# A fused Mamba and mixture-of-experts layer: the skip term moved from TensorE to VectorE, the expert ranking moved one turn earlier, and two GpSimd jobs exchanged

## The chip, the cores and the metric

The kernel runs on one NeuronCore of one Trainium2 chip, in float32 throughout. The metric is the device time in microseconds (us). Before the change the median of three runs is 1366.08 us (1365.59 to 1366.9).

## The reference, cut to what matters

Two sequences of 2048 tokens with 256 channels go through a Mamba block, a gated feed-forward, and eight experts of which each token uses the best two.

```python
u  = layernorm(layernorm(x)) * ln1_w + ln1_b
xm, z = split(u @ in_proj_w.T)                  # 512 channels each
xc = silu(causal_conv4(xm) + conv_b)
dt, Bm, Cm = split(xc @ x_proj_w.T)             # 128, 16 and 16 columns
dt = softplus(dt @ dt_proj_w.T + dt_proj_b)
for t in time:                                  # h: 512 channels x 16 states
    h = h * exp(dt[t] * A) + dt[t] * Bm[t] * xc[t]
    y[t] = sum over states of h * Cm[t]
y = (y + xc * D_skip) * silu(z)
x1 = x + y @ out_proj_w.T
x2 = x1 + (silu(gate) * a) @ ff_out_w.T         # a, gate from layernorm(x1) @ ff_proj_w.T
p = softmax(router logits); the two largest p of a token, over their sum, weigh its experts
out = x2 + sum over e of w[e] * (n @ Wa[e] @ Wb[e])   # n = layernorm(x2); residual terms left out here
```

## The kernel before, in words

The tokens are cut into 16 steps (c, b) of 256 tokens: 8 chunks of each of the 2 sequences. A step has 16 turns, one for each state s. Five stages of five neighbouring steps are interleaved in every turn: `enter` (normalisation, input projection, convolution) and `ready` (step sizes, softplus, dt times x) of the steps to come, `main` (the scan) of the present one, `back` (output projection, feed-forward) and `tail` (routing, experts) of the two that have gone by. `drive` (line 152) writes that order out for each engine: `main` part 0, then the other stages in an order that each engine's `drive` call names, then `main` part 1. A loop covers steps (2, 0) to (5, 1); what precedes the first step is `opening`, what follows the last is `closing`. Nothing is planned at run time; each engine follows its own list and waits on semaphores.

A state s passes through the engines so. ScalarE makes dA = exp(dt A) (`decay`, L801), and ScalarE or, for the states in `POOL_STATES`, GpSimd multiplies uTs by B (`weigh_u`, L789 and L559) three turns ahead. TensorE transposes that into one of three PSUM banks `psx` (`fill_bx`, L1185, 4 transposes for each half). VectorE scans (L976, two instructions a half; half 0 in part 0 and half 1 in part 1). GpSimd multiplies the scanned h by C into `hC`, a ring of 4 (L575). TensorE transposes and adds `hC` into `psy` two turns later (`sum_states`, L1204).

The skip term xc times D is made by ScalarE four products at a time into `acc` (`skip`, L771), and TensorE starts the sum in `psy` with it in turn 2 (`add_skip`, L1195). After the last state VectorE multiplies `psy` by silu(z) (`ygt`, L987, in `back` 2), TensorE transposes the result in turn 3 (L1273) into `psb` and `pst`, ScalarE copies both halves to `yg` (L841, turns 3 and 4), and TensorE projects it in turns 4 and 5 (L1068). Before TensorE may write `psb` in turn 3, ScalarE must have copied half of z out of it (L820, `main` turn 3).

The ranking of the experts: VectorE makes the logits less their maximum in `tail` 2 (lgm, L1021), ScalarE their exponential pr in `tail` 3 (L873), GpSimd ten small instructions in `tail` 3 (L616 to L641, the last writes psel), VectorE the sum and its reciprocal in `tail` 4, ScalarE the weights cw in `tail` 4 (L878), TensorE their transposes in `tail` 4 (L1298). In turns 6 to 9 TensorE makes the hidden values of two experts each (`hidden`, L1062 into `pst`), and VectorE multiplies each pair out of `pst` (L1032, turns 7 to 10); the next pair may be written only then.

Softplus is relu plus log1p(exp(-|.|)) with a correction of log1p: VectorE's L960 and L962 (`ready` 8), then on GpSimd a subtraction (L542, `ready` 8), an addition (L547, `ready` 9) and the product with xc (L551, `ready` 10). GpSimd also normalises the coming input into `xn` in `enter` 6 (L510).

Of the kernel before, what the change touches and what calls it, by code (L numbers as in the profile page):

```python
# [8 lines left out]
P = 128  # L9
T = 256  # L10
SUB = T // P
# [14 lines left out]
EPS = 1e-5  # L26
NORM_FLOOR = 1e-12
LIFT = 20
POOL_STATES = (4, 8, 14, 15)


C_CONVW, C_CONVB, C_DTB, C_DSKIP, C_ALOG = 0, NJ * TAPS, NJ * TAPS + NJ, NJ * TAPS + 2 * NJ, NJ * TAPS + 3 * NJ
# [12 lines left out]


RANK_PARTS = 9
LINKS_IN = 1
LINKS_BACK = 2
LINKS_TAIL = 2  # L50
# [132 lines left out]
def mamba_moe(nc, x, params, w_in, w_x, w_dt, w_out, w_ff, w_fo, w_a, w_b, w_r, bc_scratch, cw_scratch, out):  # L183
# [9 lines left out]
    with ctx:  # L193
# [86 lines left out]

        u = sp_l
        hg = yg
        sk = acc

        def pairs(half):
            return nx[:, half, 0:SUB * NE * NE].rearrange("p (j e f) -> p j e f", j=SUB, e=NE)
# [7 lines left out]
        pst = ctx.enter_context(nc.psum_tensor("pst", [P, 2, T], f32))  # L297

        loaded = {k: sem(f"loaded_{k}") for k in ("par", "in", "x", "dt", "out", "ff", "fo", "a", "b", "r")}
        ident_zero, ident_ready, skip_ready = sem("ident_zero"), sem("ident_ready"), sem("skip_ready")  # L300
        earlier_one, earlier_ready = sem("earlier_one"), sem("earlier_ready")
        consts_ready, state_zero, halo_zero = sem("consts_ready"), sem("state_zero"), sem("halo_zero")
        a_exp, a_ready, ln_one_ready = sem("a_exp"), sem("a_ready"), sem("ln_one_ready")
# [157 lines left out]
        def _(pool):  # L461
# [74 lines left out]

            def ready(s, m):
                b = m[1]
                if s == 8:

                    pool.wait_ge(sp_fix, count(1, m, 1))
                    nc.gpsimd.tensor_tensor(sp_l[:, :, :], sp_l[:, :, :], sp_e[:, :, :], ALU.subtract  # L542
                                            ).then_inc(sp_rest, 1)
                if s == 9:
                    pool.wait_ge(relu_done, count(2, m, 2))
                    pool.wait_ge(sp_rest, count(1, m, 1))
                    nc.gpsimd.tensor_tensor(dt[:, b], dt[:, b], sp_l[:, :, :], ALU.add).then_inc(dt_done, 1)  # L547
                if s == 10:
                    pool.wait_ge(dt_done, count(1, m, 1))
                    pool.wait_ge(xc_done, count(1, m, 1))  # L550
                    nc.gpsimd.tensor_tensor(u[:, :, :], dt[:, b], xc[:, b], ALU.mult).then_inc(u_done, 1)  # L551
# [45 lines left out]
            def tail(s, m):  # L597
                if s == 0:
# [6 lines left out]
                    pool.wait_ge(nrm_part, squared)  # L605
                    nc.gpsimd.tensor_scalar(nrm[:, 2, :], nrm[:, 1, :], float(DM), NORM_FLOOR * NORM_FLOOR, ALU.mult,
                                            ALU.max).then_inc(nrm_done, 1)
                if s == 3:


                    if is_first(m):
                        pool.wait_ge(earlier_ready, 1)
                    pool.wait_ge(pr_done, count(1, m, 1))
                    p_j = pr[:, :, :].unsqueeze(2).to_broadcast([P, SUB, NE, NE])
                    p_e = pr[:, :, :].unsqueeze(3).to_broadcast([P, SUB, NE, NE])
                    nc.gpsimd.tensor_tensor(gap, p_j, p_e, ALU.subtract).then_inc(rank_part, 1)  # L616
                    differed = value(count(RANK_PARTS, m, 1))
                    pool.wait_ge(ident_ready, 1)
                    pool.wait_ge(rank_part, differed)
                    nc.gpsimd.tensor_scalar(ahead, gap, 0.0, None, ALU.is_equal).then_inc(rank_part, 1)  # L620
                    nc.gpsimd.tensor_scalar(gap, gap, 0.0, None, ALU.is_gt).then_inc(rank_part, 1)
                    pool.wait_ge(rank_part, count(RANK_PARTS, m, 3))
                    nc.gpsimd.tensor_tensor(ahead, ahead, earlier[:, :, :].unsqueeze(1).to_broadcast([P, SUB, NE, NE]),
                                            ALU.mult).then_inc(rank_part, 1)
                    pool.wait_ge(rank_part, count(RANK_PARTS, m, 4))
                    nc.gpsimd.tensor_tensor(ahead, ahead, gap, ALU.add).then_inc(rank_part, 1)
                    pool.wait_ge(rank_part, count(RANK_PARTS, m, 5))
                    nc.gpsimd.tensor_tensor(ahead[:, :, :, 0:4], ahead[:, :, :, 0:4], ahead[:, :, :, 4:8], ALU.add
                                            ).then_inc(rank_part, 1)
                    pool.wait_ge(rank_part, count(RANK_PARTS, m, 6))  # L630
                    nc.gpsimd.tensor_tensor(ahead[:, :, :, 0:2], ahead[:, :, :, 0:2], ahead[:, :, :, 2:4], ALU.add
                                            ).then_inc(rank_part, 1)
                    pool.wait_ge(rank_part, count(RANK_PARTS, m, 7))
                    nc.gpsimd.tensor_tensor(rank[:, :, :], ahead[:, :, :, 0], ahead[:, :, :, 1], ALU.add
                                            ).then_inc(rank_part, 1)
                    ranked = value(count(RANK_PARTS, m, 8))
                    pool.wait_ge(ident_ready, 1)
                    pool.wait_ge(rank_part, ranked)
                    nc.gpsimd.tensor_scalar(rank[:, :, :], rank[:, :, :], 1.5, None, ALU.is_lt).then_inc(rank_part, 1)
                    pool.wait_ge(rank_part, count(RANK_PARTS, m, 9))  # L640
                    nc.gpsimd.tensor_tensor(psel[:, :, :], rank[:, :, :], pr[:, :, :], ALU.mult).then_inc(psel_done, 1)  # L641
# [4 lines left out]
        def _(act):  # L646
# [29 lines left out]
            def enter(s, m):  # L676
# [11 lines left out]
                    last.then_inc(uT_done, 1)  # L688
                if s in (4, 5):
                    i = s - 4  # L690
                    act.wait_ge(skip_added, count(1, m, -1))
                    act.wait_ge(filled_in, in_fill(f"x{i}", m))
                    for k in range(2):
                        j = 2 * i + k
# [7 lines left out]
                                         ).then_inc(halo_kept, 1)  # L702
                if s == 10:

                    act.wait_ge(edge_added, count(1, m, 1))
                    nc.scalar.activation(xc[:, b, :, :], acc[:, :, :], ACT.Silu).then_inc(xc_done, 1)
                    if isinstance(m[0], int) and m[0] == 0:
                        use_log_exp()
                if s == 12:
# [1 line left out]
                    act.wait_ge(filled_in, in_fill("bc", m))  # L711
                    nc.scalar.activation(bc[:, :], (pst if is_first(m) else psf)[0:2 * S, 1, :], ACT.Copy
                                         ).then_inc(bc_done, 1)
                if s == 12 and is_early(m) and not is_first(m):
                    skip(prev(m))

            def ready(s, m):
                b = m[1]
# [27 lines left out]
                if s == 8:  # L746
# [3 lines left out]
                    src = psb if is_first(m) else psf  # L750
                    nc.scalar.activation(sz[:, b, 1, :], src[:, :, :].rearrange("p k t -> p (k t)"), ACT.Copy
                                         ).then_inc(z1_copied, 1)
                if s == 12 and not is_first(m):
                    skip(m)
                if s in (13, 14):

                    j = s - 13
# [4 lines left out]
                    nc.scalar.activation(uTs[:, b, j, :], src, ACT.Copy).then_inc(uTs_done, 1)  # L762
                if s >= 13:
                    made(s - S, m)

            def skip(m):


                act.wait_ge(xc_done, count(1, m, 1 if is_last(m) else 2))
                for j in range(NJ):  # L770
                    last = nc.scalar.activation(sk[:, j, :], xc[:, m[1], j, :], ACT.Copy, scale=pcol(C_DSKIP + j))  # L771
                last.then_inc(skip_ready, 1)

            def made(turn, n):

# [85 lines left out]
            def tail(s, m):  # L861
# [3 lines left out]
                if s == 1:  # L865
# [2 lines left out]
                    nc.scalar.activation(lnn[:, :], nrm[:, 2, :], ACT.Ln, scale=float(2 ** LIFT)).then_inc(lnn_done, 1)  # L868
                    act.wait_ge(lnn_done, count(1, m, 1))
                    nc.scalar.activation(rn[:, :], lnn[:, :], ACT.Exp, scale=-0.5, bias=lift_c[:, :]).then_inc(rn_done, 1)  # L870
                if s == 3:
                    act.wait_ge(lgm_done, count(1, m, 1))
                    nc.scalar.activation(pr[:, :, :], lgm[:, :, :], ACT.Exp).then_inc(pr_done, 1)  # L873
                if s == 4:
# [7 lines left out]
                    act.wait_ge(cw_stored, count(16, m, 0))  # L882
                    nc.scalar.activation(cT[:, :], pst[0:NE, 0, :], ACT.Copy).then_inc(cT_done, 1)

            drive(act, {"else": ("tail", "back", "ready", "enter")}, enter, ready, main, back, tail)

        @block.vector
        def _(dve):
# [67 lines left out]
            def ready(s, m):  # L956
                if s == 8:

                    dve.wait_ge(sp_ln, count(1, m, 1))
                    nc.vector.scalar_tensor_tensor(out=sp_l[:, :, :], in0=sp_l[:, :, :], scalar=ln_one[:, :],  # L960
                                                   in1=sp_e[:, :, :], op0=ALU.subtract, op1=ALU.add)
                    nc.vector.tensor_scalar(sp_e[:, :, :], sp_e[:, :, :], 1.0, -1.0, ALU.add, ALU.add  # L962
                                            ).then_inc(sp_fix, 1)

            def main(s, n, part):
                b, r = n[1], ring(s)
                if part == 0:
                    dve.wait_ge(exp_done, count(S, n, s + 1))

# [72 lines left out]
        def _(pe):  # L1042
# [143 lines left out]
                                                   bxT[:, ring(s), j, c:c + P], ident[:, :])  # L1186
                last.then_inc(bx_filled, 1)

            def add_skip(n):

                pe.wait_ge(skip_ready, count(1, n, 1))
                pe.wait_ge(yg_done, count(2, n, 0))
                for j in range(SUB):
                    for i in range(NJ):
                        last = mm(psy[j][:, i * P:(i + 1) * P], sk[:, i, j * P:(j + 1) * P], ident[:, :],  # L1195
                                  is_transpose=True, start=i == 0, stop=False, skip_group_check=True)
                last.then_inc(skip_added, 1)

            def sum_states(s, n):

                pe.wait_ge(hc_done, count(S, n, s + 1))
                for j in range(SUB):
                    for i in range(NJ):
                        last = mm(psy[j][:, i * P:(i + 1) * P], hC[:, s % RC, i, j * P:(j + 1) * P], ident[:, :],  # L1204
                                  is_transpose=True, start=False, stop=s == S - 1, skip_group_check=True)
                last.then_inc(y_summed, 1)

            def main(s, n, part):
# [3 lines left out]
                    pe.wait_ge(eT_done, count(1, n, -1))  # L1212
                    gate_inputs(psb, 0, n[1]).then_inc(z0_filled, 1)
                if part == 1:
                    if s == 2:
                        add_skip(n)
                    if s >= 2:
                        sum_states(s - 2, n)

# [161 lines left out]
```

## Time and profile before

| | us |
|---|---|
| median of 3 runs | 1366.08 |
| the profiled execution | 1364.54 |
| its span, first to last instruction | 1362.8 |
| TensorE busy | 1231.1 (90%) |
| TensorE weight loads busy | 1058.5 (78%) |
| VectorE busy | 971.3 (71%) |
| ScalarE busy | 1057.8 (78%) |
| GpSimd busy | 1092.7 (80%) |
| mean granted TensorE clock | 0.976 of full |

Busy time is the time in which an engine executes something. Five overlapping stages keep all engines busy, so the shares tell little by themselves; what matters is which wait ends last in a turn. In the middle of the kernel a step takes 78.6 to 80.2 us and repeats itself closely.

### The profile page before, as it was taken

How to read it: one execution, taken by the hardware profiler on the slowest of the kernel's cores; microseconds unless marked ns; L12 is line 12 of the kernel's file. 1: busy time of each engine (PE TensorE's matmuls, PEld its weight loads, DVE VectorE, ACT ScalarE, POOL GpSimd, SP SyncE). 2: the span in 40 equal slices, each digit the busy share in tenths (PEclk: the TensorE clock that was granted, in tenths of full speed). 3: DMA queues.
4: the chain of work that ended last, by engine and by line, in shares of the span. 5: the costliest groups of instructions: out<-in, count | busy, mean ns of one | idle time of the engine just before them, and what ended most of it. 6: DMA issues, size and time to landing. Idle time of an engine off the chain costs nothing.

```text
span 1362.8 us, 24300 instructions
## 1 busy us (share of the span) xinstructions
PE 1231.1 (90%) x7680; PEld 1058.5 (78%) x7680; DVE 971.3 (71%) x1765; ACT 1057.8 (78%) x2537; POOL 1092.7 (80%) x826
## 2 busy tenths in 40 slices
PE   4587889999999999999999999999999999898986
PEld 3366777887878787787878878787887878787875
DVE  2486868778786876878687786868778686878621
ACT  3798898888787878878788887878788787878420
POOL 3389798888888888888888888888888888788721
PEclk8798899999999999999999999999999999999998
DMA  1411102111121111112111111211121021202001
GB/s 65 171 47 40 39 26 77 40 47 63 48 79 46 57 40 56 56 48 79 49 56 40 66 46 48 79 48 56 40 79 47 33 71 48 71 24 73 30 32 47
DMA packets 29223, 75.08 MB, mean 55 GB/s; under 512 B 3104, under 2 KB 15776, under 8 KB 26528
## 3 DMA queue, kind: packets, MB, share of 16 engines
q1 hardware_dynamic: 29088, 73.41, 16.1%
q8 instruction: 69, 1.13, 0.3%
q14 instruction: 66, 0.54, 0.1%
HBM read 64.61 MB, written 4.59 MB: 51 GB/s over the span
## 4 chain that ended last, share of the span: by engine, by line
PE 72%; ACT 9%; DVE 7%; issue 5%; POOL 2%; DMA 0%; DVEq 0%; ACTq 0%; POOLq 0%; SPq 0%
PE psx L1185 12%; PE psy L1204 12%; PE psb L1062 8%; PE psb L1068 8%; PE pst L1068 8%; PE pst L1062 6%; DVE h L976 3%; ACT dA L801 2%; PE psf L1062 2%; ACT bxT L789 2%; PE psf L1153 2%; PE psf L1159 2%; PE psf L1094 2%; PE psb L1159 2%; PE psf L1105 2%
## 5 line engine op out<-in xcount | busy, mean ns | idle before, releaser
L976 DVE TENSOR_TENSOR_SCAN h<-dA,state,psx 128x256 f32<-128x256 f32 x1024 | 681.4, 726 | 112.8 <-PE psx L1185 99.2
L575 POOL TENSOR_TENSOR hC<-h,bC 128x1024 f32<-128x1024 f32 x256 | 606.1, 2372 | 96.0 <-DVE h L976 73.8
L801 ACT ACTIVATE dA<-dt,neg_a 128x256 f32<-128x256 f32 x1024 | 434.3, 500 | 0.0
L1185 PE MATMUL psx<-ident,bxT 128*128 128x128 f32 x2048 | 307.0, 276 | 25.2 <-DVE h L976 15.2
L789 ACT ACTIVATE bxT<-uTs,BT 128x512 f32<-128x512 f32 x384 | 254.1, 717 | 67.4 <-PE psx L1185 65.8
L1185 PEld LDWEIGHTS psx<-ident,bxT 128*128 128x128 f32 x2048 | 246.2, 143 | 68.5 <-issue 24.3
L1204 PE MATMUL psy<-ident,hC 128*128 128x128 f32 x2048 | 267.6, 274 | 1.5 <-POOL hC L575 1.5
L1204 PEld LDWEIGHTS psy<-ident,hC 128*128 128x128 f32 x2048 | 235.2, 143 | 4.5 <-POOL hC L575 1.7
L559 POOL TENSOR_TENSOR bxT<-uTs,BT 128x1024 f32<-128x1024 f32 x64 | 121.5, 1898 | 32.0 <-PE psx L1185 32.0
L1062 PE MATMUL psb<-nT,w_ff_sb 128*128 128x256 f32 x496 | 121.8, 388 | 12.9 <-ACT yg L814 11.7
L1062 PE MATMUL pst<-eT,w_a_sb 128*128 128x256 f32 x448 | 107.2, 382 | 14.2 <-DVE cbc L1032 14.2
L1062 PEld LDWEIGHTS psb<-nT,w_ff_sb 128*128 128x128 f32 x496 | 89.3, 190 | 34.7 <-ACT yg L814 18.0
L1068 PE MATMUL pst<-w_b_sb,cbc 128*128 128x256 f32 x480 | 110.8, 379 | 0.0
L1062 PEld LDWEIGHTS pst<-eT,w_a_sb 128*128 128x128 f32 x448 | 81.8, 190 | 26.5 <-DVE cbc L1032 15.6
L1068 PEld LDWEIGHTS pst<-w_b_sb,cbc 128*128 128x128 f32 x480 | 90.1, 190 | 11.7
L483 POOL TENSOR_SCALAR nx<-x,mv,rstd 128x256 f32<-128x256 f32 x64 | 77.6, 1223 | 22.9 <-ACT rstd L662 22.9
L1068 PE MATMUL psb<-w_out_sb,yg 128*128 128x256 f32 x256 | 65.8, 402 | 26.3 <-ACT yg L841 26.3
L952 DVE SCALAR_TENSOR_TENSOR acc<-psf,par,acc 128x255 f32<-128x255 f32 (+1 forms) x180 | 73.6, 472 | 17.3 <-ACT halo L701 17.3
L1068 PEld LDWEIGHTS psb<-w_out_sb,yg 128*128 128x128 f32 x256 | 49.1, 197 | 38.6 <-ACT yg L841 30.6
L999 DVE TENSOR_TENSOR yg<-yg,psb 128x512 f32<-128x512 f32 x31 | 21.3, 688 | 66.3 <-PE psb L1062 66.3
L542 POOL TENSOR_TENSOR sp_l<-sp_l,sp_e 128x1024 f32<-128x1024 f32 x16 | 37.8, 2363 | 35.5 <-DVE sp_e L962 35.5
L1062 PE MATMUL psf<-uT,w_in_sb 128*128 128x256 f32 x240 | 60.0, 394 | 4.7 <-ACT uT L686 2.5
(148 smaller groups left out, 1633.7 us busy)
## 6 DMA issues: line engine op xcount, KB each, us to landing
bC<-bc_scratch SPq DMA_DIRECT2D x64, 512.0 KB, 3.8
cbc<-cw_scratch SPq DMA_DIRECT2D x16, 1024.0 KB, 4.7
xf<-in_x SPq DMA_DIRECT2D x16, 256.0 KB, 2.7
xk<-xn SPq DMA_DIRECT2D x16, 256.0 KB, 4.3
xb<-in_x SPq DMA_DIRECT2D x16, 256.0 KB, 4.2
out<-x SPq DMA_DIRECT2D x16, 256.0 KB, 2.2
w_in_sb<-in_w_in SPq DMA_DIRECT2D x1, 1024.0 KB, 5.2
w_ff_sb<-in_w_ff SPq DMA_DIRECT2D x1, 1024.0 KB, 5.9
```

Of the source, the lines that this page charges most:

```text
L483: last = nc.gpsimd.tensor_scalar(dst[:, j, :], src[:, j, :], mv[k][:, j, 0:1], rstd[k + 1][:, j:j + 1], ALU.subtract, ALU.mult)
L559: nc.gpsimd.tensor_tensor(bxT[:, ring(s)], uTs[:, n[1]], BT[:, n[1], :, s:s + 1].to_broadcast([P, SUB, DI]), ALU.mult).then_inc(bxT_pool, 1)
L575: nc.gpsimd.tensor_tensor(hC[:, s % RC], h[:, ring(s)], bC[:, g % RINGG, s % G:s % G + 1, :].to_broadcast([P, NJ, T]), ALU.mult).then_inc( ...
L789: last = nc.scalar.activation(bxT[:, ring(s), j, :], uTs[:, n[1], j, :], ACT.Copy, scale=BT[:, n[1], j, s:s + 1])
L801: last = nc.scalar.activation(dA[:, s % RA, j, :], dt[:, n[1], j, :], ACT.Exp, scale=neg_a[:, j, s:s + 1])
L952: nc.vector.scalar_tensor_tensor(out=acc[:, j, tap:], in0=x_bank(i, m)[:, j % 2, 0:T - tap], scalar=pcol(C_CONVW + j * TAPS + k), in1=acc[ ...
L976: last = nc.vector.tensor_tensor_scan(h[:, r, j, :], dA[:, s % RA, j, :], psx[bx_bank(fill)][:, k, :], state[:, b, j, s:s + 1], ALU.mult, ...
L1062: last = mm(dst[:, i, :], w[:, k, c:c + P], rhs[:, k, :], start=k == 0, stop=k == kt - 1)
L1068: last = mm(dst[:, j, :], lhs[:, k, j * P:(j + 1) * P], w[:, k, :], start=k == 0, stop=k == kt - 1)
L1159: last = mm(dst[:, :, :].rearrange("p k t -> p (k t)"), uT[:, b, k, j * P:(j + 1) * P], w_in_sb[:, k, DI:2 * DI], start=k == 0, stop=k == ...
L1185: last = nc.tensor.transpose(psx[bx_bank(fill)][:, k, j * P:(j + 1) * P], bxT[:, ring(s), j, c:c + P], ident[:, :])
L1204: last = mm(psy[j][:, i * P:(i + 1) * P], hC[:, s % RC, i, j * P:(j + 1) * P], ident[:, :], is_transpose=True, start=False, stop=s == S - ...
```

## The change

`POOL_STATES` gets state 6: GpSimd makes its bxT and ScalarE no longer does. ScalarE's `skip` and TensorE's `add_skip` go; the first state's sum starts `psy`. VectorE adds xc times D to `hC` of state 4, in place, in part 1 of turn 6, ahead of its scans, and TensorE's sum of state 4 waits for it. VectorE does the subtraction of softplus in `ready` 9. `tail` 3 of ScalarE and GpSimd (pr and the ranking) becomes `tail` 2, and ScalarE's order of the stages changes in turns 2 and 4.

```diff
-POOL_STATES = (4, 8, 14, 15)
+POOL_STATES = (4, 6, 8, 14, 15)
+SKIP = 4
...
 (GpSimd, ready)
-                if s == 8:
-                    pool.wait_ge(sp_fix, count(1, m, 1))
-                    nc.gpsimd.tensor_tensor(sp_l[:, :, :], sp_l[:, :, :], sp_e[:, :, :], ALU.subtract
-                                            ).then_inc(sp_rest, 1)
 (GpSimd, tail; ScalarE, tail)
-                if s == 3:
+                if s == 2:
 (ScalarE, enter)
                 if s in (4, 5):
-                    act.wait_ge(skip_added, count(1, m, -1))
+                    act.wait_ge(xc_done, count(1, m, 0))
                 if s == 10:
+                    act.wait_ge(skip_added, count(1, m, -1))
-                if s == 12 and is_early(m) and not is_first(m):
-                    skip(prev(m))
 (ScalarE, ready; skip itself goes too)
-                if s == 12 and not is_first(m):
-                    skip(m)
 (ScalarE)
-            drive(act, {"else": ("tail", "back", "ready", "enter")}, ...)
+            drive(act, {2: ("back", "ready", "enter", "tail"), 4: ("back", "tail", "ready", "enter"),
+                        "else": ("tail", "back", "ready", "enter")}, ...)
 (VectorE, ready)
+                if s == 9:
+                    dve.wait_ge(sp_fix, count(1, m, 1))
+                    nc.vector.tensor_tensor(sp_l[:, :, :], sp_l[:, :, :], sp_e[:, :, :], ALU.subtract).then_inc(sp_rest, 1)
 (VectorE, main, first thing)
+                if part == 1 and s == SKIP + 2:
+                    dve.wait_ge(hc_done, count(S, n, SKIP + 1))
+                    for j in range(NJ):
+                        last = nc.vector.scalar_tensor_tensor(out=hC[:, SKIP % RC, j, :], in0=xc[:, b, j, :],
+                                                              scalar=pcol(C_DSKIP + j), in1=hC[:, SKIP % RC, j, :],
+                                                              op0=ALU.mult, op1=ALU.add)
+                    last.then_inc(skip_added, 1)
 (TensorE; add_skip and its call in turn 2 go)
             def sum_states(s, n):
+                if s == 0:
+                    pe.wait_ge(yg_done, count(2, n, 0))
+                if s == SKIP:
+                    pe.wait_ge(skip_added, count(1, n, 1))
...
-                                  is_transpose=True, start=False, stop=s == S - 1, skip_group_check=True)
+                                  is_transpose=True, start=s == 0 and i == 0, stop=s == S - 1, skip_group_check=True)
```

## Rows read from the trace of the kernel before

**Rows 1.** Part 4 of the page: shares of the chain that ended last.

```profile
PE 72%; ACT 9%; DVE 7%; issue 5%; POOL 2%; DMA 0%; DVEq 0%; ACTq 0%; POOLq 0%; SPq 0%
```

**Rows 2.** Waits of the run: engine line <- releaser: us in total, times, longest.

```profile
PE psb L1068 <- ACT yg L841: 26.3, 16, 3.2
...
PE pst L1062 <- DVE cbc L1032: 14.2, 12, 1.2
```

**Rows 3.** Timeline of TensorE, one step: start us, us, engine line op [idle before].

```profile
766.86 1.04 PE L1195 MATMUL psy<-ident,acc 128*128 128x128 f32 x8
767.73 1.04 PE L1204 MATMUL psy<-ident,hC 128*128 128x128 f32 x8
...
769.48 0.60 PE L1273 MATMUL psb<-ident,ygt 128*128 128x128 f32 x4
...
772.10 1.89 PE L1062 MATMUL psf<-uT,w_in_sb 128*128 128x256 f32 x8
775.57 1.99 PE L1068 MATMUL psb<-w_out_sb,yg 128*128 128x256 f32 x8 [1.58 <-ACT yg L841]
...
789.73 1.99 PE L1062 MATMUL pst<-eT,w_a_sb 128*128 128x256 f32 x8 [1.20 <-DVE cbc L1032]
```

**Rows 4.** Timeline of ScalarE, same step.

```profile
768.72 0.61 ACT L820 ACTIVATE sz<-psb 128x512 f32<-128x512 f32 x1
...
771.60 1.33 ACT L789 ACTIVATE bxT<-uTs,BT 128x512 f32<-128x512 f32 x2
772.83 1.70 ACT L801 ACTIVATE dA<-dt,neg_a 128x256 f32<-128x256 f32 x4
...
774.94 0.57 ACT L841 ACTIVATE yg<-pst 128x512 f32<-128x512 f32 x1
```

**Rows 5.** Timeline of GpSimd, same step.

```profile
763.42 2.38 POOL L575 TENSOR_TENSOR hC<-h,bC 128x1024 f32<-128x1024 f32 x1
...
769.63 0.39 POOL L616 TENSOR_TENSOR nx<-pr 128x128 f32<-128x128 f32 x1
...
773.82 0.22 POOL L641 TENSOR_TENSOR psel<-rank,pr 128x16 f32<-128x16 f32 x1
...
778.64 1.90 POOL L559 TENSOR_TENSOR bxT<-uTs,BT 128x1024 f32<-128x1024 f32 x1
...
783.15 2.45 POOL L510 TENSOR_SCALAR xn<-xf,mv,rstd 128x256 f32<-128x256 f32 x2
```

**Rows 6.** Timeline of VectorE, same step.

```profile
765.12 0.72 DVE L1021 TENSOR_TENSOR lgm<-lg,mx 128x16 f32<-128x16 f32 x1
...
783.17 0.69 DVE L992 TENSOR_TENSOR x<-xk,psb 128x512 f32<-128x512 f32 x1 [1.24 <-PE psb L1068]
...
784.87 1.65 DVE L952 SCALAR_TENSOR_TENSOR acc<-psf,par,acc 128x255 f32<-128x255 f32 x4
786.45 2.65 DVE L976 TENSOR_TENSOR_SCAN h<-dA,state,psx 128x256 f32<-128x256 f32 x4
789.01 0.66 DVE L1032 TENSOR_TENSOR cbc<-cbc,pst 128x512 f32<-128x512 f32 x1
```

**Rows 7.** Line 960 in the whole run: ns minimum/median/maximum, first and last start.

```profile
L960 DVE SCALAR_TENSOR_TENSOR sp_l<-sp_l,ln_one,sp_e x16: 1269/2642/3369, 37.3 to 1185.2; 128x1024 f32<-128x1024 f32 x16
```

**Rows 8.** Timeline of VectorE, then of TensorE, turns 9 to 11 of another step.

```profile
721.06 2.65 DVE L976 TENSOR_TENSOR_SCAN h<-dA,state,psx 128x256 f32<-128x256 f32 x4
...
725.34 0.60 PE L1185 MATMUL psx<-ident,bxT 128*128 128x128 f32 x4
```

**Rows 9.** A stretch: us, busy PE PEld DVE ACT POOL, granted clock, DMA share, GB/s.

```profile
220.00:224.00 4.00, 3.87 (x15) 3.17 (x16) 3.89 (x9) 4.00 (x12) 3.24 (x2) 0.67 0.42 134
```

**Rows 10.** Timeline of TensorE at two of its longer waits.

```profile
220.13 2.61 PE L1068 MATMUL psb<-w_out_sb,yg 128*128 128x256 f32 x8 [2.00 <-ACT yg L841]
...
1169.85 3.40 PE L1068 MATMUL psb<-w_out_sb,yg 128*128 128x256 f32 x8 [3.21 <-ACT yg L841]
```

**Rows 11.** A group: line engine op xcount, busy us, mean ns, idle before, releaser.

```profile
L542 POOL TENSOR_TENSOR sp_l<-sp_l,sp_e 128x1024 f32<-128x1024 f32 x16 | 37.8, 2363 | 35.5 <-DVE sp_e L962 35.5
```

More of the change, by code:

```diff
@@ L285, in mamba_moe @@
         hg = yg
-        sk = acc
         def pairs(half):
@@ L299, in mamba_moe @@
         loaded = {k: sem(f"loaded_{k}") for k in ("par", "in", "x", "dt", "out", "ff", "fo", "a", "b", "r")}
-        ident_zero, ident_ready, skip_ready = sem("ident_zero"), sem("ident_ready"), sem("skip_ready")
+        ident_zero, ident_ready = sem("ident_zero"), sem("ident_ready")
         earlier_one, earlier_ready = sem("earlier_one"), sem("earlier_ready")
@@ L764, in ready @@
                     made(s - S, m)
[L766 to L772, printed above, removed]
             def made(turn, n):
@@ L870, in tail @@
                     nc.scalar.activation(rn[:, :], lnn[:, :], ACT.Exp, scale=-0.5, bias=lift_c[:, :]).then_inc(rn_done, 1)
-                if s == 3:
+                if s == 2:
                     act.wait_ge(lgm_done, count(1, m, 1))
@@ L883, in tail @@
                     nc.scalar.activation(cT[:, :], pst[0:NE, 0, :], ACT.Copy).then_inc(cT_done, 1)
-            drive(act, {"else": ("tail", "back", "ready", "enter")}, enter, ready, main, back, tail)
+            drive(act, {2: ("back", "ready", "enter", "tail"), 4: ("back", "tail", "ready", "enter"),
+                        "else": ("tail", "back", "ready", "enter")}, enter, ready, main, back, tail)
         @block.vector
@@ L1187, in fill_bx @@
                 last.then_inc(bx_filled, 1)
[L1189 to L1197, printed above, removed]
             def sum_states(s, n):
+                if s == 0:
+                    pe.wait_ge(yg_done, count(2, n, 0))
+                if s == SKIP:
+                    pe.wait_ge(skip_added, count(1, n, 1))
                 pe.wait_ge(hc_done, count(S, n, s + 1))
@@ L1214, in main @@
                 if part == 1:
-                    if s == 2:
-                        add_skip(n)
                     if s >= 2:
```

## The prediction

> **What bounds the kernel now.** I read the chain first. TensorE holds 72% of it and every other engine under a tenth [rows 1]: in the middle of the kernel TensorE's list is the path, and the others count where they make TensorE wait. The list of waits gives those places [rows 2]: 16 waits for ScalarE's copy of yg (26.3 us together) and 12 for VectorE's expert product (14.2 us). The timelines of one step show them again, 1.58 us in turn 4 and 1.20 us in turn 7 [rows 3].
>
> In turn 4 the copy of yg stands on ScalarE behind the expert weights, and these behind the ranking, which GpSimd ends at 774.04 [rows 4, 5]. In turn 7 the path goes the other way. TensorE's projection lets VectorE start its addition at 783.17; two normalisation statistics, four convolution taps, four scans and the expert product follow without a gap to 789.67, and TensorE goes on at 789.73 [rows 3, 6]. From 783.17 to 789.73 **VectorE is the path**. Whatever is put into that stretch is paid in full.
>
> I work in the time of this one step, which 12 of the 16 resemble (the 12 waits of [rows 2]).
>
> **Part by part.** *No skip transposes.* Eight transposes go; by the starts of their block and the next they hold TensorE 0.87 us [rows 3]. But three blocks later TensorE writes `psb`, from which ScalarE copies z from 768.72 to 769.33, and TensorE begins at 769.48 [rows 3, 4]: it was there just in time. ScalarE's list ahead of that copy is not shortened (its skip products stood in turn 12, state 6 in turn 3). So the 0.87 us becomes a new wait for L820: I count 0, and 0.87 at best. ScalarE's exponential now stands ahead of that copy and costs 0.1.
>
> *Ranking in turn 2, state 6 on GpSimd.* ScalarE loses bxT of state 6, 1.23 us from start to start [rows 4], and in turn 4 copies yg before the expert weights. It reaches the copy after dA at about 773.2 and ends it by 773.9. TensorE's input projection starts at 772.10 and, at 1.73 us a block of eight (the 0.16 is overlap), leaves it at 773.83. The wait of 1.58 shrinks to about 0.1. Gain: **1.5 us a step** (0 to 1.58).
> GpSimd's list grows here. The exponential is ready at 766.1, so the ten instructions, 4.4 us from 769.63 to 774.04 [rows 5], end at 770.6. Behind them queue hC of state 2, the new bxT of state 6 (1.86, as the one at 778.64), hC of 3 and 4 (2.33 each), bxT of 8, hC of 5, and then xn, two instructions of 1.2 us. Summed, xn runs from **783.65 to 786.05**, against 783.15 to 785.6 now. TensorE needs bxT of state 6 at 777.3 and has it at 774.9; it needs the product of state 2 at 776.5 and has it at 773.0. These are covered by over 2 us.
>
> *The skip on VectorE.* Four instructions, 256 elements each, one input scaled. The nearest row is four taps, 1.58 us by starts [rows 6], but a tap has one input in PSUM. With both in SBUF there is L960: 1269 ns at best for 1024 elements, 2642 in the middle [rows 7]. The difference is GpSimd: the subtraction lgm of 16 elements took 0.72 us and ended at 765.84, as the product of 763.42 did on GpSimd (765.80) [rows 5, 6]. A VectorE instruction with two SBUF inputs stands while GpSimd executes a tensor_tensor. No row shows it against a tensor_scalar, which xn is. Bounds: nothing blocks, 1.6 us; both halves of xn block, 1.6 + 2.4 = 4.0 us. The taps end at 786.45 - 1.5 = 784.95, xn at 786.05, so 1.1 us of blocking is the value I take, since xn too reads SBUF: **2.7 us a step**, all on the stretch where VectorE is the path.
> The Trainium skill, "SBUF — State Buffer", section "Who interferes with whom", says that a VectorE instruction with two SBUF inputs contends with a GpSimd instruction that reads SBUF, whichever it is, and that the later one blocks fully. Lgm agrees as to tensor_tensor; for tensor_scalar the page alone speaks. By it the block is the 1.1 us, without it 0.
> Queued behind the skip on VectorE are the scans of turn 6, and TensorE's sum of state 4, its next fills of `psx` and its expert block all wait.
>
> *Subtraction on VectorE.* 1024 elements from two SBUF inputs: 1.17 us free, up to 2.6 blocked [rows 7]. It delays the scans of [rows 8] from 721.06. Their first two would end 1.7 us later than 722.4, at 724.1, and TensorE asks for them at 725.34: hidden, by 1.2 us. The addition on GpSimd comes 0.2 us later than now. If that cover were gone it would cost up to 1.4 us a step. I take 0. GpSimd saves 2.36 us and its wait for L962 [rows 11], off the path.
>
> *Clock.* TensorE will stand for some 4 of 6 us around turn 6: 2.3 us for the skip, 0.4 for a scan, 1.6 for the expert product. Now it stands 1.20 and 1.58 us at a time, and the eight matmuls behind each take 1.99 us [rows 3]. After a stand of 2.00 us the same eight took 2.61, and the stretch from 220 shows a granted clock of 0.67, so partly the lower level of 1.2 GHz; after 3.21 us they took 3.40 [rows 9, 10]. Between 0 (the slow part falls into a stand) and 1.4 I take **0.6 us a step**.
>
> **The sum.** A middle step: 0.1 is within the 1.5, so -1.5 + 2.7 + 0 + 0.6 = +1.8, times 12 = +21.6. The others: in the opening ScalarE's four skip products (1.6 by starts, as the four dA of [rows 4]) and half of the subtraction (2.36 [rows 11] to 1.17) leave the path, -2.8. The first step pays the skip and saves the subtraction on GpSimd, +0.5; the second has a shorter wait for yg, and pays the skip, +1. The last two have no convolution: their waits for yg of 3.2 [rows 10] and about 2.7 (which [rows 2] leaves when the others are taken off) shrink to 0.7, the first with 1.4 of slow clock, and the skip costs 0.85 each: -3.0 and -1.2. Sum of these -5.5. Together **+16** on the profiled execution's 1364.54 (span 1362.8 and 1.7 around it), 1380.6; the median lay 1.5 above that execution, so 1382.
>
> **Rivals.**
> 1. *GpSimd's tensor_scalar does not block.* Then a step is -1.5 + 1.6 = +0.1 and the rest -5.5: -4, 1362, faster. With the clock's 0.6 it is +3, 1369. For it: no row shows such a block. Against: the operand side is the same as that of the blocking product. 0.23, half of it with the clock.
> 2. *VectorE has room.* The skip fits between other work, the transposes' 0.87 and the 1.5 are kept: -2.4 times 16, 1328. It needs slack on VectorE from 783.17 to 789.67, and there is none; decides if TensorE's wait in turn 7 does not grow. 0.05.
> 3. *The clock halves in each step, and both halves of xn block.* 1.3 and 0.8 more: +1.8 becomes +3.9, times 12 less 5.5 is +41, 1408. 0.07.
> 4. *Ranking ahead of state 2's product holds the scans.* VectorE's scan of state 5 could start at 772.6 and gets that product at 773.0. Were the list on GpSimd 3 us later, the taps of turn 5 and TensorE's input block behind them would be late and the gain of 1.5 lost: +1.5 times 12 on top, 1400. Against: by my sum these taps wait for ScalarE until 775.4, a second after the scan. 0.05.
> 5. *The change does less than it says*: ScalarE still reaches yg late and the skip is not blocked: like 1, no gain, +1.6 a step, 19 less 5.5 is +14, 1380. Near the forecast; 0.05.
>
> The forecast itself has 0.55: 1382; 1375 without the clock and 1392 with all of it bound it. A difference under 0.2% (2.7 us) can't be told from none in this kernel. Faster: half of rival 1, rival 2 and a rest for what I mis-sized, 0.21. Same: 0.1. Slower: 0.69. The range 1360 to 1400 takes in rival 1 and leaves out 2 and 3.
>
> **What would show it.** Right: turn 4's wait for L841 near 0.1; a new wait of TensorE for L820 of 0.8 in turn 3; the four skip instructions at 0.4 us each but the first of 1.5 us, while xn executes; TensorE's waits in turns 6 and 7 at 4 us together, and clock under 1 in some of these stretches; middle steps at 79.7 to 80.5 us instead of 78.7. Wrong: a middle step under 78.6 us; skip instructions of 0.4 us beside xn (rival 1); no longer wait in turn 7 (rival 2); VectorE's scan of state 5 waiting for GpSimd (rival 4).

## The result, and the profile after

| | before | after |
|---|---|---|
| median, us | 1366.49 (4 runs) | 1375.97 (4 runs) |
| profiled span, us | 1362.8 | 1373.6 |
| VectorE busy | 971.3 (71%) | 1033.2 (75%) |
| ScalarE busy | 1057.8 (78%) | 1014.7 (74%) |

The ratio is 1.0068, interval 1.005 to 1.0085: **slower, by 9.5 us**; forecast were 1382 and 1360 to 1400. One run of early_silu below took 1825.36 us at a granted clock of 0.652 and is left out of its figures. The shares of the chain, against [rows 1], have moved from TensorE to VectorE:

```profile
PE 61%; DVE 15%; ACT 9%; issue 8%; DMA 1%; POOL 1%; DVEq 0%; ACTq 0%; POOLq 0%; SPq 0%
```

The waits of the whole run (columns as in [rows 2]) say where. Of the 26.3 us for yg 2.0 are left, all in the last two steps and behind them, and 26.3 us for the skip stand in their place, one wait in each of the 16 steps; the wait for the expert product stays.

```profile
PE psy L1194 <- DVE hC L959: 26.3, 16, 2.8
PE psx L1181 <- DVE h L972: 17.0, 28, 2.5
PE pst L1058 <- DVE cbc L1028: 15.2, 14, 1.2
```

TensorE's timeline in the step of [rows 3], which now runs 2.4 us later as a whole:

```profile
772.15 0.63 PE L1261 MATMUL psb<-ident,ygt 128*128 128x128 f32 x4 [0.77 <-issue]
...
776.54 1.99 PE L1064 MATMUL psb<-w_out_sb,yg 128*128 128x256 f32 x8
...
787.48 0.60 PE L1181 MATMUL psx<-ident,bxT 128*128 128x128 f32 x4
789.54 1.09 PE L1194 MATMUL psy<-ident,hC 128*128 128x128 f32 x8 [1.46 <-DVE hC L959]
790.76 0.66 PE L1181 MATMUL psx<-ident,bxT 128*128 128x128 f32 x4
792.62 1.99 PE L1058 MATMUL pst<-eT,w_a_sb 128*128 128x256 f32 x8 [1.20 <-DVE cbc L1028]
```

The projection that waited 1.58 waits no more; the block of the skip's sum waits 1.46. The reader should also see what did not change: both eights of 256 columns take 1.99 us, as in [rows 3]. The 0.77 in front of L1261 is the z copy of the prediction, which the waits list as "issue": ScalarE's timeline ends that copy at 772.05, and TensorE starts at 772.15. Of ScalarE:

```profile
768.41 0.24 ACT L856 ACTIVATE pr<-lgm 128x16 f32<-128x16 f32 x1
...
771.44 0.61 ACT L803 ACTIVATE sz<-psb 128x512 f32<-128x512 f32 x1
...
775.90 0.59 ACT L824 ACTIVATE yg<-pst 128x512 f32<-128x512 f32 x1
```

VectorE's stretch of [rows 6], and GpSimd beside it, with the skip between the taps and the scans:

```profile
785.90 1.65 DVE L936 SCALAR_TENSOR_TENSOR acc<-psf,par,acc 128x255 f32<-128x255 f32 x4
787.47 1.94 DVE L959 SCALAR_TENSOR_TENSOR hC<-xc,par,hC 128x256 f32<-128x256 f32 x4
789.34 2.65 DVE L972 TENSOR_TENSOR_SCAN h<-dA,state,psx 128x256 f32<-128x256 f32 x4
791.91 0.66 DVE L1028 TENSOR_TENSOR cbc<-cbc,pst 128x512 f32<-128x512 f32 x1
...
786.16 2.46 POOL L509 TENSOR_SCALAR xn<-xf,mv,rstd 128x256 f32<-128x256 f32 x2
```

xn lies over the skip until 788.62, and the skip takes no more than 1.94 us; in the 12 middle steps it takes 1.79 to 2.16. Where no GpSimd instruction lies beside it, in the second step, it takes 1.67:

```profile
157.14 1.67 DVE L959 SCALAR_TENSOR_TENSOR hC<-xc,par,hC 128x256 f32<-128x256 f32 x4
```

The last two steps have no convolution, so VectorE comes to the skip while GpSimd executes two products, both tensor_tensor, L553 (which makes bxT) and then L569:

```profile
1179.76 4.37 DVE L959 SCALAR_TENSOR_TENSOR hC<-xc,par,hC 128x256 f32<-128x256 f32 x4
...
1178.67 1.90 POOL L553 TENSOR_TENSOR bxT<-uTs,BT 128x1024 f32<-128x1024 f32 x1
1180.52 2.53 POOL L569 TENSOR_TENSOR hC<-h,bC 128x1024 f32<-128x1024 f32 x1
...
1184.19 1.57 PE L1194 MATMUL psy<-ident,hC 128*128 128x128 f32 x8 [2.23 <-DVE hC L959]
...
1187.34 3.78 PE L1058 MATMUL pst<-eT,w_a_sb 128*128 128x256 f32 x8 [0.68 <-DVE cbc L1028]
```

Here the skip takes 2.7 us more than alone, and the eight matmuls after the two stands take 3.78 instead of 1.99: the granted clock from 1187 to 1191 is 0.50, so TensorE is at the lower of its two levels, 1.2 GHz instead of 2.4. In the last step the skip takes 4.34, and the eight after it 2.10. The mean granted clock from 1182 to 1305 is 0.96; from 1179 to 1295 of the kernel before it is 0.99.

Step by step (from one start of the z product on VectorE to the next) the spans' difference of 10.8 us is made up so:

| part | forecast | measured |
|---|---|---|
| opening and first step | -2.8 and +0.5 | +0.9 (135.79 to 136.70) |
| second step | +1 | +0.3 |
| the 12 middle steps | +21.6 | +3.7 (950.3 to 954.0) |
| last two steps | -3.0, -1.2 | +2.3, +2.0 |
| tail | not in the sum | +1.7 |
| sum | +16.1 | +10.8 (the parts are rounded) |

### The profile page after: what moved, and what is told of

Its sections match the earlier page's. It is cut to its first block, busy times and chain, and to the rows that moved or that the text cites. A ratio compares the mean times of both kernels' runs of the same rounds, so it can differ in the third digit from the quotient of the medians.

```text
span 1373.6 us, 24039 instructions
## 1 busy us (share of the span) xinstructions
PE 1222.1 (89%) x7552; PEld 1044.8 (76%) x7552; DVE 1033.2 (75%) x1845; ACT 1014.7 (74%) x2441; POOL 1087.2 (79%) x826
## 3 DMA queue, kind: packets, MB, share of 16 engines
q1 hardware_dynamic: 29088, 73.41, 16.1%
## 4 chain that ended last, share of the span: by engine, by line
PE 61%; DVE 15%; ACT 9%; issue 8%; DMA 1%; POOL 1%; DVEq 0%; ACTq 0%; POOLq 0%; SPq 0%
PE psx L1181 10%; PE psy L1194 10%; PE pst L1064 8%; PE psb L1064 7%; DVE h L972 7%; PE psb L1058 6%; PE psf L1058 3%; PE pst L1058 3%; ACT dA L784 3%; PE psf L1090 2%; PE psf L1149 2%; PE psf L1101 2%; DVE hC L959 2%; DVE acc L936 2%; PE psb L1155 1%
## 5 line engine op out<-in xcount | busy, mean ns | idle before, releaser
L569 POOL TENSOR_TENSOR hC<-h,bC 128x1024 f32<-128x1024 f32 x256 | 606.9, 2375 | 112.1 <-DVE h L972 108.7
L1194 PE MATMUL psy<-ident,hC 128*128 128x128 f32 x2048 | 270.4, 276 | 27.8 <-DVE hC L959 26.3
L772 ACT ACTIVATE bxT<-uTs,BT 128x512 f32<-128x512 f32 x352 | 232.8, 716 | 67.6 <-PE psx L1181 66.0
L553 POOL TENSOR_TENSOR bxT<-uTs,BT 128x1024 f32<-128x1024 f32 x80 | 151.9, 1899 | 28.1 <-PE psx L1181 28.1
L482 POOL TENSOR_SCALAR nx<-x,mv,rstd 128x256 f32<-128x256 f32 x64 | 77.6, 1221 | 24.6 <-ACT rstd L656 24.6
L791 ACT ACTIVATE state<-h 128x4 f32<-128x4 f32 x256 | 51.0, 205 | 30.6 <-DVE h L972 30.5
L753 ACT ACTIVATE uTs<-psf 128x512 f32<-128x512 f32 x30 | 17.9, 597 | 63.2 <-PE psf L1163 63.2
L541 POOL TENSOR_TENSOR dt<-dt,sp_l 128x1024 f32<-128x1024 f32 x16 | 37.8, 2362 | 29.7 <-DVE sp_l L950 29.7
```

What stands on the lines that cost most here:

```text
L482: last = nc.gpsimd.tensor_scalar(dst[:, j, :], src[:, j, :], mv[k][:, j, 0:1], rstd[k + 1][:, j:j + 1], ALU.subtract, ALU.mult)
L553: nc.gpsimd.tensor_tensor(bxT[:, ring(s)], uTs[:, n[1]], BT[:, n[1], :, s:s + 1].to_broadcast([P, SUB, DI]), ALU.mult).then_inc(bxT_pool, 1)
L569: nc.gpsimd.tensor_tensor(hC[:, s % RC], h[:, ring(s)], bC[:, g % RINGG, s % G:s % G + 1, :].to_broadcast([P, NJ, T]), ALU.mult).then_inc( ...
L772: last = nc.scalar.activation(bxT[:, ring(s), j, :], uTs[:, n[1], j, :], ACT.Copy, scale=BT[:, n[1], j, s:s + 1])
L791: nc.scalar.activation(state[:, n[1], :, s:s + 1], h[:, ring(s), :, T - 1:T], ACT.Copy).then_inc(state_saved, 1)
```

## The experiments

Ratios are against runs of the kernel before on the same chip, taken together with each experiment; their medians are 1364.3 to 1366.3 us, so two times of different experiments can differ by 2 us for that alone. A middle step is 78.7 us before and 79.05 after. In every kernel three to five of the twelve middle steps are 1 to 3 us longer; step times and ranges below are those of the others.

**undo_skip**: everything but the skip, which stays on ScalarE and TensorE.

```diff
-if part == 1 and s == SKIP + 2:     # VectorE: xc*D onto hC of state 4
+if s == 12 and not is_first(m): skip(m)   # ScalarE, and add_skip on TensorE
```

> The changed kernel with the skip term back on ScalarE and TensorE; the ranking in turn 2, state 6 on GpSimd and the subtraction on VectorE stay. Theory (the skip on VectorE is paid in full in turn 6, the rest gains some 1.5 us a step): TensorE's wait of about 1.4 us for the skip goes, the wait for yg stays away, a middle step 77.3 us against 78.7 before and 79.2 changed, and about 1343 us in all. Rival A (the three other edits bring nothing, what was gained in turn 4 came from shorter TensorE lists): 1366. Rival B (a part of the loss is the subtraction on VectorE): 1350 to 1360.

1345.76 (1343.76 to 1347.14), ratio 0.9865, 0.9849 to 0.9882. The rest of the change wins 18.6 us. A middle step takes 77.1 to 77.6, TensorE's waits in turn 4 of the middle steps and for the skip are gone, and what is left in turns 4 to 7 is the expert product's:

```profile
777.17 1.99 PE L1062 MATMUL pst<-eT,w_a_sb 128*128 128x256 f32 x8 [1.20 <-DVE cbc L1032]
```

Against the whole change the skip costs 30.2 us, and 28.0 if each time is taken against its own kernel before; by the two spans 28.2, of it 18.9 in the 12 middle steps (1.6 each), 4.5 in the last but one, 2.5 in the second, but only 0.2 in the last (67.19 to 67.37). There the step is 1.8 us longer than before (65.39) without any skip. VectorE's expert product waits there for the transfer that brings the expert weights, and TensorE for that product:

```profile
1232.83 0.69 DVE L1032 TENSOR_TENSOR cbc<-cbc,pst 128x512 f32<-128x512 f32 x1 [2.07 <-DMA cbc<-cw_scratch]
1233.57 2.75 PE L1062 MATMUL pst<-eT,w_a_sb 128*128 128x256 f32 x8 [1.93 <-DVE cbc L1032]
```

The kernel before has no such wait in that step, and the whole change has none either: there the skip takes up that time.

**skip_only**: the kernel before with the skip's move alone.

```diff
+if part == 1 and s == SKIP + 2:     # VectorE
-if s == 12 and not is_first(m): skip(m)
```

> The kernel before with nothing but the skip term on VectorE in turn 6. Theory: no gain in turn 4, as the copy of yg still waits for the ranking; the four instructions cost 1.6 to 1.9 us in each of the 12 middle steps, and the last two are not blocked by a product on GpSimd, since that one has ended: about 1390 us. TensorE still stands 0.8 us for the copy of z in turn 3. Rival (the skip transposes were worth their 0.87 us a step): 1377.

1394.89 (1389.77 to 1396.91), ratio 1.0223, 1.0196 to 1.0251. The skip costs 30.6 us without the others too. The totals agree within 2.5 us, but they are not made up of the same parts, so that they agree shows only that the skip's cost does not need the other edits. A middle step takes 80.25, 1.6 more than before (17.0 for the twelve). No skip is slowed here from the second step on: 1.66 or 1.67 us in each middle step, and 1.64 in the last two, where GpSimd's product has ended at 1201.90 as expected:

```profile
1202.34 1.64 DVE L960 SCALAR_TENSOR_TENSOR hC<-xc,par,hC 128x256 f32<-128x256 f32 x4
```

In exchange the opening with the first step is 3.7 us longer than before (139.44), the second step 2.7, and the last 3.6, with a wait for yg of 4.9 instead of 2.7.

**rank_only**: ranking in turn 2 with ScalarE's new orders, nothing else.

```diff
-if s == 3:
+if s == 2:
+drive(act, {2: ("back", "ready", "enter", "tail"), 4: ("back", "tail", "ready", "enter"), ...
```

> The kernel before with nothing but the ranking in turn 2 and ScalarE's new orders in turns 2 and 4; state 6 stays on ScalarE. Theory: ScalarE reaches the copy of yg only 0.3 to 0.4 us earlier, since its bxT of state 6 stands ahead of it, so the wait in turn 4 falls from 1.58 to about 1.2 us; more in the last two steps, whose waits of 3 us were the ranking's alone: about 1357 us. Rival (the ranking alone was the wait, state 6 is idle weight): wait near 0.1 and 1343.

1357.26 (1354.67 to 1357.93), ratio 0.9956, 0.994 to 0.9973. The wait for yg is 18.7 us in all where it was 26.3, 1.1 in a middle step instead of 1.5: ScalarE still makes bxT of state 6 ahead of it.

**state6_only**: state 6 on GpSimd, nothing else.

```diff
-POOL_STATES = (4, 8, 14, 15)
+POOL_STATES = (4, 6, 8, 14, 15)
```

> The kernel before with nothing but state 6 scaled by GpSimd. Theory (GpSimd makes it in turn 3 ahead of the ranking, whose end is what the copy of yg waits for): 1.9 us more of TensorE's wait in turn 4 in 14 steps, and a slow clock behind some of these waits: about 1393 us, 3.4 us of wait a step. Rival (ScalarE's relief counts more): 1350 to 1366.

1403.41 (1401.43 to 1405.37), ratio 1.0278, 1.0261 to 1.0295: slower than I expected by 10. GpSimd now makes bxT ahead of the ranking, and by that the ranking, the expert weights and yg end 1.9 us later. GpSimd, ScalarE and TensorE, turns 3 and 4:

```profile
788.44 1.90 POOL L559 TENSOR_TENSOR bxT<-uTs,BT 128x1024 f32<-128x1024 f32 x1
790.29 0.41 POOL L616 TENSOR_TENSOR nx<-pr 128x128 f32<-128x128 f32 x1
...
794.49 0.22 POOL L641 TENSOR_TENSOR psel<-rank,pr 128x16 f32<-128x16 f32 x1
...
795.21 0.49 ACT L879 ACTIVATE cw<-psel,rden 128x8 f32<-128x8 f32 x2 [3.12 <-DVE rden L1027]
795.61 0.57 ACT L842 ACTIVATE yg<-pst 128x512 f32<-128x512 f32 x1
...
796.24 2.70 PE L1069 MATMUL psb<-w_out_sb,yg 128*128 128x256 f32 x8 [3.46 <-ACT yg L842]
```

The wait is 3.46 instead of 1.58, and part of the time is the lower level behind it: 2.70 us here, and 3.78 one step earlier behind a stand of 2.87. Two stands of one length in this run show that the length alone does not settle it:

```profile
549.56 1.99 PE L1069 MATMUL psb<-w_out_sb,yg 128*128 128x256 f32 x8 [2.86 <-ACT yg L842]
...
879.10 3.62 PE L1069 MATMUL psb<-w_out_sb,yg 128*128 128x256 f32 x8 [2.86 <-ACT yg L842]
```

The granted clock is 1.00 from 549 to 551 and 0.55 from 879 to 882. So the same edit costs 38 us alone and, once the ranking stands ahead of it, gains 10 or more on top of rank_only (1345.8 to 1347.0 against 1357.3). Ranking and state 6 are one edit in two places.

**sub_only**: softplus' subtraction on VectorE, nothing else.

```diff
-nc.gpsimd.tensor_tensor(sp_l[:, :, :], sp_l[:, :, :], sp_e[:, :, :], ALU.subtract)
+nc.vector.tensor_tensor(sp_l[:, :, :], sp_l[:, :, :], sp_e[:, :, :], ALU.subtract)
```

> The kernel before with nothing but softplus' subtraction on VectorE. Theory: covered in every middle step (VectorE waits for TensorE in turns 10 to 12), 1.2 us less in the opening: within 2 us of before, 1363. Rival (VectorE's added 1.9 us a step reach TensorE in turns 9 and 10): 1370 or more.

1364.35 (10 runs, 1359.19 to 1368.17), ratio 0.9997, 0.9982 to 1.0012: no difference.

**undo_both**: undo_skip, with the subtraction on GpSimd again as well.

```diff
-if s == 9:  # VectorE
-    nc.vector.tensor_tensor(sp_l[:, :, :], sp_l[:, :, :], sp_e[:, :, :], ALU.subtract)
+if s == 8:  # GpSimd
+    nc.gpsimd.tensor_tensor(sp_l[:, :, :], sp_l[:, :, :], sp_e[:, :, :], ALU.subtract)
```

> Ranking in turn 2 and state 6 on GpSimd alone: both the skip and softplus' subtraction are as in the kernel before. Beside the run with only the skip undone (1345.8) it differs by where the subtraction runs. Theory: the subtraction's place is worth nothing (alone it measured 0.9997), so 1346 (1344 to 1348). Rival: with state 6 on GpSimd its queue is fuller, the subtraction there makes dt and the later hC late, 3 to 8 us slower: 1349 to 1354, with waits of psy for POOL hC.

1347.05 (1345.78 to 1348.83), ratio 0.9863, 0.9842 to 0.9884: nothing is seen of the subtraction's place on a fuller GpSimd either.

**skip7**: the whole change, with the skip one turn later, onto state 5.

```diff
-SKIP = 4
+SKIP = 5
```

> The changed kernel with the skip added to state 5's product, in turn 7 and so behind the expert product of that turn, instead of state 4's in turn 6. Theory (only the place on the path makes the skip dear): VectorE has some slack between turn 7 and turn 9, so a middle step loses 0.3 to 0.8 us of the skip's 1.9 and takes about 78.0 us; TensorE's wait for the skip in turn 6 goes: about 1356 us. Rival (VectorE's work counts wherever it stands): as the changed kernel, 1376.

1359.46 (10 runs, 1357.37 to 1361.02), ratio 0.9961, 0.9951 to 0.9972. One turn is worth 14 us by the spans (16.5 by the medians). A middle step takes 77.8 to 78.3, and the last two steps 70.64 and 66.08 where the whole change has 74.94 and 67.37. It costs 14 more than undo_skip, so turn 7 has no room for all of the skip either.

**skip7_z0**: skip7, and ScalarE copies the first half of z one turn earlier.

```diff
-if part == 0 and s == 3:
+if s == 2:      # in part 1, ahead of made
     nc.scalar.activation(sz[:, n[1], 0, :], psb..., ACT.Copy).then_inc(z0_copied, 1)
```

> The changed kernel with the skip in turn 7 on state 5's product, and ScalarE's copy of the first half of z in turn 2, ahead of that turn's scaling and decay, instead of in turn 3. Theory (the 0.87 us of the skip transposes were lost to that copy alone): TensorE's wait of 0.8 us in turn 3 goes, a middle step 77.4 us instead of 78.2, about 1347 us. Rival (the next wait on ScalarE, yg or the relu, takes its place): 1357 to 1360.

1356.3 (1354.67 to 1358.21), ratio 0.9932, 0.9915 to 0.9949. The wait of 0.8 for the copy is gone and a middle step gains only 0.2 on average. Two others on ScalarE stand in its place:

```profile
768.86 1.99 PE L1058 MATMUL psf<-uT,w_in_sb 128*128 128x256 f32 x8 [0.15 <-ACT uT L680]
771.03 1.99 PE L1064 MATMUL psb<-w_out_sb,yg 128*128 128x256 f32 x8 [0.18 <-ACT yg L824]
```

The expected 77.4 us a step and 1347 were wrong; the rival, other waits on ScalarE and 1357 to 1360, was near. These two make up 0.33 of the 0.8; the rest was not traced.

**undo_skip_z0**: the same copy in undo_skip.

> The changed kernel with the skip back on ScalarE and TensorE, and ScalarE's copy of the first half of z one turn earlier. Middle steps then wait only 2.4 for cbc, 1.4 for the gate product, 1.1 for ScalarE's bxT and 0.7 for scans in two steps; there is no wait for the z copy that the earlier copy could take away. Theory: no gain, 1346 (1343 to 1349), with another 0.5 to 1 us wait for bxT or a scan in a middle step since ScalarE's copy stands ahead of them. Rival: the copy still moves the turns behind it forward and each middle step gains 0.3 (as 0.2 to 0.3 in the pair with the skip in turn 7), 1342.

1341.84 (6 runs, 1338.02 to 1348.63), ratio 0.9823, 0.9797 to 0.9848: the fastest that was run, and faster than both kernels of this case. No gain was expected, and the rival's 1342 was met; but this interval ends where that of undo_skip begins, and 3.0 of the 4.6 us by which the middle steps of the two traces differ lie in one step (80.07 to 77.11), so how much the copy gives is not settled.

**early_silu**: the whole change, without the wait for the skip ahead of Silu in the two opening steps, where its count is 0.

```diff
-act.wait_ge(skip_added, count(1, m, -1))
+skips = count(1, m, -1)
+if not (isinstance(skips, int) and skips == 0):
+    act.wait_ge(skip_added, skips)
```

> The changed kernel with one wait less: in the two opening steps ScalarE does not wait for skip_added ahead of Silu (the count it waits for is 0 there, so nothing is ordered by it). Theory: with two waits ahead of Silu the activation table is loaded behind them, on the path (49.14 in the changed kernel, 43.52 in the kernel before, where it lay in the idle time before POOL's edge); with one wait the load goes back into the idle time. In the profile the loads then start near 18.9 and 43.5 us, and xc (Silu) follows its taps without 1.28 us between; the opening ends 1.3 to 2.5 us earlier, and the time is 1374 (1373 to 1375) against the changed kernel's 1376. Rival: the loads move, but the opening is held by something else (the weights' DMAs, the halved clock), and the time stays at 1376. Rival 2: the place of the load has nothing to do with the wait; loads stay at 49.1.

1373.44 (1371.08 to 1376.43), ratio 1.0054, 1.0034 to 1.0074, which is not told apart from the whole change. But the load of the activation table did move. ScalarE in the whole change, then here:

```profile
49.14 1.28 ACT L701 ACT_TABLE_LOAD   x1 [4.50 <-POOL acc L533]
50.43 1.06 ACT L701 ACTIVATE xc<-acc 128x1024 f32<-128x1024 f32 x1
```

```profile
44.44 1.28 ACT L703 ACT_TABLE_LOAD   x1
48.89 1.06 ACT L703 ACTIVATE xc<-acc 128x1024 f32<-128x1024 f32 x1 [3.17 <-POOL acc L533]
```

With a second wait ahead of the activation the load ran behind the wait, and with one it ran in the idle time before it, as it did in the kernel before (43.52). The activation comes 1.5 us earlier, and the opening ends 0.2 earlier (136.49): TensorE's wait for ScalarE's bxT falls from 9.2 to 7.9, and one of 1.5 for GpSimd's bxT is new. So the move of the load is real and not what holds the opening: the first rival.

**ports**: the kernel before with a piece behind its end: eight instructions like the skip's on VectorE, beside nothing, four tensor_scalar and two tensor_tensor on GpSimd; then the last two again with one input in PSUM.

```diff
+for phase, kind in enumerate(("sbuf", "sbuf", "sbuf", "psum", "psum")):
+    dve.wait_ge(bench_pool, phase + 1)
+    both(kind, 8).then_inc(bench_dve, 1)
```

> The kernel before, with a measurement behind its end: VectorE executes eight of the skip's instructions (256 elements) five times: with both inputs in SBUF beside nothing or the start of it, beside four tensor_scalar of GpSimd of 256 elements (as xn), beside two tensor_tensor of 1024 elements (as hC), and with one input in PSUM beside the same two. Theory now (from the changed kernel's trace): a tensor_scalar slows the eight by at most 0.3 us in all, a tensor_tensor holds them until it ends, some 4.7 us on top of 3.3, and with an input in PSUM nothing holds them: eight in 3.3 us. Rival A (what I wrote before: any GpSimd instruction that reads SBUF holds them): beside tensor_scalar 4.9 us on top. Rival B (the long skips of the last steps came from something else, such as the wait for state 4's product): 3.3 us in every case.

VectorE, phase by phase (rows of four), and what GpSimd did beside the second, third and fourth:

```profile
6014.28 1.67 DVE L1069 SCALAR_TENSOR_TENSOR sp_e<-xc,par,hC 128x256 f32<-128x256 f32 x4 [3.35 <-POOL un L648]
...
6018.57 1.90 DVE L1069 SCALAR_TENSOR_TENSOR sp_e<-xc,par,hC 128x256 f32<-128x256 f32 x4 [1.04 <-POOL un L653]
6020.39 1.80 DVE L1069 SCALAR_TENSOR_TENSOR sp_l<-xc,par,hC 128x256 f32<-128x256 f32 x4
6025.41 5.75 DVE L1069 SCALAR_TENSOR_TENSOR sp_e<-xc,par,hC 128x256 f32<-128x256 f32 x4 [3.23 <-POOL un L653]
...
6033.80 1.66 DVE L1073 SCALAR_TENSOR_TENSOR sp_e<-psf,par,hC 128x256 f32<-128x256 f32 x4 [1.05 <-POOL un L653]
...
6039.45 1.66 DVE L1073 SCALAR_TENSOR_TENSOR sp_e<-psf,par,hC 128x256 f32<-128x256 f32 x4 [2.43 <-POOL un L653]
...
6018.45 6.03 POOL L656 TENSOR_SCALAR bxT<-xf,mv,rstd 128x256 f32<-128x256 f32 x4
...
6025.28 4.81 POOL L659 TENSOR_TENSOR dA<-h,bC 128x1024 f32<-128x1024 f32 x2
...
6033.68 4.84 POOL L656 TENSOR_SCALAR bxT<-xf,mv,rstd 128x256 f32<-128x256 f32 x4
```

Four instructions take 1.67 alone, 1.90 and 1.80 beside tensor_scalar, 5.75 beside tensor_tensor, and 1.66 beside either with an input in PSUM. Each of the two tensor_tensor holds one instruction until it ends (2.48 and 2.56 us), and the other two take the usual time. That settles rival 1's mechanism for VectorE. GpSimd pays as well: its four tensor_scalar take 6.03 beside instructions with two SBUF inputs and 4.84 beside those with an input in PSUM. It was executed once. The kernel as a whole took 6046 us, at a granted clock of 1.00, since each matmul in it took about three times as long (the fills of `psx` 897 ns on average against 276 before). Why is open; the rows above stand where TensorE has finished, and the scans in that kernel take 734 ns against 726, so VectorE's times can be compared.

## Why the prediction was right in its sum and wrong in its parts

**No skip transposes: right.** The 0.87 came back as a wait of 0.77 for the z copy, in the turn that was named. skip7_z0 adds that the copy was not the only one.

**Ranking and state 6: right, 1.5 forecast.** From the z product on VectorE to the projection TensorE took 12.22 us (763.35 to 775.57 before) and takes 10.77: a gain of 1.45. Rival 4's wait of the scans exists, 0.58 for `hC`, and costs nothing that TensorE's list shows. GpSimd's list came out as summed: xn starts 20.4 us after the z product, and 20.3 was forecast. That the two edits need each other was not in the prediction.

**Subtraction: right, 0.** sub_only and undo_both.

**The skip: the place right, the term mis-sized.** 2.7 was forecast, 1.6 of work and 1.1 of blocking by xn. The way from the projection to the expert block in turn 7 took 14.16 us and takes 16.08: 1.92. Of that the work is 1.67 and the blocking 0.27; ports shows 0.23 and 0.13 for the same pair of operations. The step that failed is "1.1 us of blocking is the value I take": xn does lie 1.15 us over the skip, and the skip does not stand for it. The Trainium skill, "SBUF — State Buffer", section "Who interferes with whom", says that a VectorE instruction with two SBUF inputs contends with a GpSimd instruction that reads SBUF, and that the one that comes later is blocked fully. The measurement decides: it is so with tensor_tensor (5.75 us) and not with tensor_scalar (1.90 and 1.80).

**Clock: 0.6 forecast, 0 in the middle.** TensorE stands 1.46 and 1.20 us there, shorter than the 2.00 of [rows 10], and the eights behind take 1.99; the waits in turns 6 and 7 are 2.7 together where some 4 were forecast. With a skip of 2.7 the stand would have been longer; this term hung on the one before.

So a middle step was worth +0.3 on average and not +1.8, near the first form of rival 1 (+0.1). By its own sign, middle steps of 79.7 to 80.5 us, the forecast was missed: they take 79.05.

**The other steps: wrong in sign, by 12.6 us.** The waits for yg in the last two steps did shrink, from 3.21 and 2.7 to 0.68 each. But "the skip costs 0.85 each" took no account of what GpSimd executes there: products, of the kind that the prediction itself had argued from [rows 5, 6] to block. The skip took 4.37 and 4.34 us, and the steps came out at +2.3 and +2.0 instead of -3.0 and -1.2. For the last but one undo_skip and skip7 confirm it: 70.43 and 70.64 where the whole change has 74.94. For the last one they do not: undo_skip takes 67.19 there. What the sum left out in that step is the transfer of the expert weights, which ends last once the wait for yg has shrunk. Single traces differ there, too: early_silu, which is the whole change but for one wait in the opening, takes 69.31 in its last step.

The -2.8 of the opening did not show: with the first step it came out 0.9 longer. ScalarE's products are gone, but it waits 1.48 for TensorE instead, and TensorE waits 2.5 for the first skip. The load of the table accounts for 0.2. sub_only, which moves the subtraction alone, gains 0.4 there (135.35), and skip_only, which takes ScalarE's products away and adds the skip, is 3.7 longer. Two kernels without the skip end it at 135.01 (undo_skip) and 137.48 (undo_both). Which wait holds the opening is open.

The tail's +1.7 was not in the sum. TensorE's wait for the expert weights there is 3.1 instead of 1.4. It is also 3.1 in undo_skip, undo_both, skip_only, skip7 and undo_skip_z0, but 1.7 in early_silu, which has all the edits of the change, and 1.4 or 1.5 in the other kernels. It follows none of the edits, and its cause is open.

The 1382 was 6 us too high, and that is luck: two errors, -17.9 in the middle and +12.6 outside it, nearly cancelled. Even the sign had luck in it. With the middle as measured and the rest as forecast the sum would have been -1.8. What the prediction argued and the runs do show is why the skip is dear: it sits where VectorE is the path. The rest of the change alone wins 18.6 us, with the skip in turn 6 the kernel loses 9.5, and with it in turn 7 it wins 4.9.

## What to carry to other kernels

Before work is moved to an engine, find the stretches in which that engine is the path, and put it elsewhere: one turn later it cost half (14 us instead of 28). Price it at every place where it runs, last steps and opening too, by what the neighbouring engine executes at that time, and ask which wait ends last once the present one has gone. When a queue gets a new item, look what urgent item stands behind it; the same item may cost 38 us or gain 10.

## What the runs showed of the hardware

VectorE reading two SBUF inputs slows by 8 to 14% beside GpSimd's tensor_scalar in the bench (1.67 to 1.80 and 1.90), by 7 to 29% in the middle steps (1.79 to 2.16), and stands until the end of its tensor_tensor; one input in PSUM frees it from both (1.66). GpSimd's four tensor_scalar take 6.03 instead of 4.84 in the same encounter. A second wait ahead of an activation, met from the start, moved the load of its table, 1.28 us, from idle time onto ScalarE's path. Stands of TensorE of up to 1.58 us in the middle steps of the kernels before and after were followed by eights of 1.99 us. Longer ones were followed by either: in the kernel before 2.00 by 2.61 and 3.21 by 3.40; in state6_only 2.86 once by 1.99 and once by 3.62; and in the kernel after, in the second step, 2.79 by a block of eight transposes at its usual 1.09.

```profile
158.86 1.09 PE L1194 MATMUL psy<-ident,hC 128*128 128x128 f32 x8 [2.79 <-DVE hC L959]
```
